# Squares and half of the Newton products of the first stage moved from ScalarE and VectorE to GpSimd

## The reference

```
def sensitivity(r, mu, sigma):
    return jnp.exp(-(1.0 / r - 1.0 / mu) ** 2 / (2.0 * sigma * sigma))   # MU = 1, SIGMA = 0.5
msg     = z @ W + B                                   # z: layer norm of x
sens    = sensitivity(dist_matrix, MU, SIGMA)         # dist_matrix: adj, 1354 x 1354
weights = jnp.where(dist_matrix < CUTOFF, sens, 0.0)  # CUTOFF = 1
x1      = x + weights @ msg
```

## Time and profile before

| | |
|---|---|
| median of three runs | 573.3 us |
| profiled execution | 573.15 us |
| its span, first to last instruction | 571.4 us |
| mean granted TensorE clock | 0.94 |
| busy over the span | PE 492.5, VectorE 387.3, ScalarE 271.6, GpSimd 118.1 us |
| first sum added to x (L1402) | 42.61 us |
| first gates turned (L1481) | 59.45 us |

### The profile page before, as it was taken

One profiled execution on the slowest core, in us unless ns is written; L12 is line 12 of the kernel. 1 busy time (PEld: TensorE's weight loads), 2 busy tenths in 40 slices (PEclk: granted clock), 3 DMA queues, 4 the chain that ended last, 5 costly groups with the idle time before them and its releaser, 6 DMA issues.

```text
span 571.4 us, 6186 instructions
## 1 busy us (share of the span) xinstructions
PE 492.5 (86%) x1889; PEld 306.4 (54%) x1889; DVE 387.3 (68%) x715; ACT 271.6 (48%) x445; POOL 118.1 (21%) x181
## 2 busy tenths in 40 slices
PE   5564879677879999999889998998978799999997
PEld 4322535344546645455444443445545687788896
DVE  2989987756586722267568868778856966666664
ACT  5988694758765421222422122111236544454553
POOL 3000000000010000000000058730103455555554
PEclk9696699889799999999999998999988999999999
DMA  8960000000000010000000013210000000000000
GB/s 284 317 170 1 1 0 0 1 1 0 1 1 1 5 45 1 0 2 0 1 0 1 28 49 103 65 30 1 0 5 2 0 2 0 20 1 2 19 1 13
DMA packets 13076, 16.76 MB, mean 29 GB/s; under 512 B 2007, under 2 KB 8410, under 8 KB 13038
## 3 DMA queue, kind: packets, MB, share of 16 engines
q1 hardware_dynamic: 13038, 16.30, 9.1%
HBM read 15.60 MB, written 0.69 MB: 29 GB/s over the span
## 4 chain that ended last, share of the span: by engine, by line
PE 56%; DVE 24%; ACT 10%; issue 8%; POOL 1%; DVEq 0%; POOLq 0%; ACTq 0%
PE bank L1220 9%; PE bank L886 7%; PE bank L888 7%; PE bank L887 7%; PE bank L1050 4%; PE bank L1168 3%; DVE pr_ring L1818 3%; PE bank L1019 2%; PE bank L1209 2%; DVE y_units L1379 2%; DVE y_units L1368 2%; PE bank L915 2%; DVE t_units L1374 2%; DVE hr_ring L1634 2%; DVE y_units L1389 1%
## 5 line engine op out<-in xcount | busy, mean ns | idle before, releaser
L1220 PE MATMUL bank<-pr_ring,hW 128*128 128x512 f32 (+3 forms) x198 | 95.5, 568 | 7.2 <-DVE pr_ring L1818 6.7
L1818 DVE SCALAR_TENSOR_TENSOR pr_ring<-adjT,regR,bank 128x512 f32<-128x512 f32 (+3 forms) x99 | 64.9, 680 | 29.5 <-PE bank L1209 27.8
L1929 DVE TENSOR_TENSOR adjT<-adjT,bank 128x512 f32<-128x512 f32 (+1 forms) x66 | 41.2, 624 | 45.5 <-PE bank L1324 24.0
L866 ACT ACTIVATE adjT<-bank 128x512 f32<-128x512 f32 (+1 forms) x66 | 36.2, 549 | 54.1 <-PE bank L888 54.1
L886 PE MATMUL bank<-z3hi,w13hi 128*128 128x512 f32 (+4 forms) x132 | 50.8, 385 | 8.2 <-DVE pr_ring L1933 3.2
L1220 PEld LDWEIGHTS bank<-pr_ring,hW 128*128 128x128 f32 (+1 forms) x198 | 35.7, 197 | 37.0 <-issue 17.8
L915 PE MATMUL bank<-y_units,msg 128*128 128x512 f32 (+3 forms) x66 | 33.3, 638 | 20.5 <-DVE y_units L1389 20.5
L888 PE MATMUL bank<-z3hi,w13lo 128*128 128x512 f32 (+4 forms) x132 | 49.4, 374 | 0.0
L887 PE MATMUL bank<-z3lo,w13hi 128*128 128x512 f32 (+4 forms) x132 | 49.0, 371 | 0.0
L1019 PE MATMUL bank<-hr_ring,W2s 128*128 128x512 f32 (+1 forms) x96 | 46.2, 569 | 0.0
L548 POOL TENSOR_TENSOR prr_ring<-adjT,adjTr 128x512 fp32r<-128x512 f32 (+4 forms) x34 | 36.0, 1060 | 48.8 <-ACT adjTr L858 46.8
(11 more groups left out here) (272 smaller groups left out, 1039.3 us busy)
## 6 DMA issues: line engine op xcount, KB each, us to landing
stage<-in_w SPq DMA_DIRECT2D x8, 341.0 KB, 3.0
adjT<-in_adjT SPq DMA_DIRECT2D x1, 2560.0 KB
adjT<-in_adjT SPq DMA_DIRECT2D x1, 1650.0 KB
adjT<-in_adjT SPq DMA_DIRECT2D x3, 512.0 KB, 5.7
adjT<-in_adjT SPq DMA_DIRECT2D x1, 1024.0 KB
W1f<-in_W SPq DMA_DIRECT2D x1, 1024.0 KB, 11.9
stage<-in_w SPq DMA_DIRECT2D x3, 256.0 KB
xT<-in_xT SPq DMA_DIRECT2D x1, 677.0 KB, 3.8
```

Of the source, the lines that this page charges most:

```text
L866: nc.scalar.activation(s1_buf(q)[0:r, 0:w], B_H1[q % 2][0:r, 0:w], ACT.Silu).then_inc(s["s_silu"], 1)
L1220: nc.tensor.matmul(B_ACC[:, 0:w], hW[0:r, j, k * P:(k + 1) * P], ring[0:r, 0:w], start=(k == 0 and j == 0), stop=(k == K - 1 and j == T - ...
L1818: nc.vector.scalar_tensor_tensor(out=pr_ring[0:r, 4 + p % R_RING, 0:w], in0=adjT[0:r, j, cols(c)], scalar=g_col[0:r, j, k:k + 1], in1=B_F[ ...
L1929: nc.vector.tensor_tensor(sg, sg, B_GATE1[n % 2][0:r, 0:w], ALU.mult).then_inc(s["s_gated"], 1)
```

## The change

GpSimd takes the squares of units 2 to 17, as a product of the adjacency with itself (L520 of the new kernel), and the products t = r*y of the eight units 2, 4, ..., 16 (L526). ScalarE keeps the squares of units 0 and 1, VectorE the products of units 0, 1 and the odd ones. The logarithm of a unit waits for GpSimd's square, and the Newton step of an even unit for GpSimd's product. GpSimd's 24 new instructions stand in one fixed order between its constants and its diagonals. In ScalarE's and VectorE's straight code the order of the tasks is written anew, with unit 6 now taken ahead of `x1(0)`; in the tables the entries "sq" and the even "mult" are gone and nothing else moves.

```
+OWN = 2
+def on_pool(g):
+    return g >= OWN and g % 2 == 0
...
 ACT0 = {
-    0: [("sq", 9), ("ln", 9), ("arg", 7), ("exp", 7), ("inv", 9)], 2: [("arg", 8), ("sq", 10), ("ln", 10), ("inv", 10)], 3: [("exp", 8)],
+    0: [("ln", 9), ("arg", 7), ("exp", 7), ("inv", 9)], 2: [("arg", 8), ("ln", 10), ("inv", 10)], 3: [("exp", 8)], 4: [("arg", 9), ("exp", 9)],
...
 DVE0 = {
-    0: [("sign", 8), ("cut", 7), ("mult", 8)], 1: [("step", 8), ("sign", 9)], 2: [("v",), ("mult", 9)], 3: [("step", 9), ("cut", 8)],
+    0: [("sign", 8), ("cut", 7)], 1: [("step", 8), ("sign", 9)], 2: [("v",), ("mult", 9)], 3: [("step", 9), ("cut", 8)],
...
+            def square(g):                     # GpSimd
+                c, a, _ = unit(g)
+                if c:
+                    at(pool, f"adjT_in{c}", 32)
+                elif a < 6:
+                    at(pool, f"adjT_first{a // 2}", 16)
+                else:
+                    at(pool, "adjT_in0", 32)
+                at(pool, "gnn_mm", g - RINGY + 1)
+                pool.tensor_tensor(unit_y(g), unit_adj(g), unit_adj(g), ALU.mult).then_inc(s["pool_sq"], 1)
+            def product(g):
+                pool.wait_ge(s["newton_s"], g + 1)
+                at(pool, "newton_y", g - RINGT + 1)
+                pool.tensor_tensor(unit_t(g), unit_adj(g), unit_y(g), ALU.mult).then_inc(s["newton_p"], 1)
+            square(2)
+            square(3)
+            square(4)
+            product(2)
+            square(5)
...
+            square(16)
+            square(17)
+            product(16)
...
             def rec_log(g):
-                act.wait_ge(s["rec_sq"], g + 1)
+                if g < OWN:
+                    act.wait_ge(s["rec_sq"], g + 1)
+                else:
+                    act.wait_ge(s["pool_sq"], g - OWN + 1)
...
             def newton_step(g):
-                at(dve, "newton_t", g + 1)
+                if on_pool(g):
+                    at(dve, "newton_p", g // 2)
+                else:
+                    at(dve, "newton_t", (g + 3) // 2)
```

More of the change, by code:

```diff
@@ L117 @@
[L117 to L121, removed]
@@ new lines @@
+    9: [("cut", 11), ("step", 12)], 10: [("sign", 13), ("mult", 13)], 11: [("x1", 1), ("center", 1, 1), ("step", 13)], 13: [("scale", 1, 1)],
+    15: [("rank", 1), ("sign", 14), ("turn", 1)], 16: [("cut", 12)], 17: [("cut", 13), ("x2", 0)], 18: [("step", 14), ("sign", 15)],
+    19: [("center", 2, 0), ("mult", 15), ("step", 15), ("sign", 16)], 20: [("cut", 14), ("step", 16)], 21: [("cut", 15), ("sign", 17), ("mult", 17)],
+    22: [("scale", 2, 0), ("step", 17), ("cut", 16)], 23: [("diag", 0), ("cut", 17)], 25: [("x1", 2), ("center", 1, 2), ("diag", 1)],
@@ L506, in _ @@
             pool.tensor_copy(GT0[:, :, :].rearrange("p i n -> p (i n)"), zero[:, 0:1].to_broadcast([P, 2 * CW])).then_inc(s["pad_zero"], 1)
+            def square(g):
[17 more added lines that the diff above has]
+            square(5)
+            square(6)
+            product(4)
+            square(7)
+            square(8)
+            product(6)
+            square(9)
+            product(8)
+            square(10)
+            square(11)
+            product(10)
+            square(12)
+            square(13)
+            product(12)
+            square(14)
+            square(15)
+            product(14)
+            square(16)
+            square(17)
+            product(16)
             pool.wait_ge(s["w_ready"], UNITS)
@@ L1610, in weights_low @@
                 nc.vector.tensor_tensor(W1lo[:, half, :], W1f[:, half, :], W1hi[:, half, :].bitcast(F32), ALU.subtract).then_inc(s["W1_lo"], 1)
[L1612 removed]
+            side(("sign", 0))
+            side(("mult", 0))
+            side(("step", 0))
+            side(("sign", 1))
+            side(("mult", 1))
+            side(("step", 1))
+            rows_step(0)
+            side(("sign", 2))
+            rows_step(1)
+            message(0)
+            side(("sign", 3))
+            side(("mult", 3))
+            message(1)
+            side(("step", 2))
+            message(2)
+            side(("cut", 0))
+            side(("step", 3))
+            side(("sign", 4))
+            side(("cut", 1))
+            side(("sign", 5))
+            side(("mult", 5))
+            side(("cut", 2))
+            dve.wait_ge(s["gate_in"], 32)
+            nc.vector.tensor_tensor(gate_bias[:, 0, :], gate_bias[:, 0, :], gate_bias[:, 1, :], ALU.add).then_inc(s["bgs_set"], 1)
+            side(("step", 4))
+            side(("step", 5))
+            side(("cut", 3))
+            side(("sign", 6))
+            dve.wait_ge(s["ffn0_in"], 80)
+            nc.vector.tensor_copy(b2hi[:, :], b2x[:, :]).then_inc(s["b2_split"], 1)
+            side(("cut", 4))
+            at(dve, "b2_split", 1)
+            nc.vector.tensor_tensor(b2lo[:, :], b2x[:, :], b2hi[:, :].bitcast(F32), ALU.subtract).then_inc(s["b2_split"], 1)
+            side(("cut", 5))
+            side(("step", 6))
             weights_low(0)
[L1614 to L1615 removed]
+            side(("x1", 0))
+            side(("center", 1, 0))
             weights_low(1)
[L1617 to L1625 removed]
+            side(("sign", 7))
+            side(("mult", 7))
+            side(("scale", 1, 0))
+            side(("cut", 6))
+            side(("rank", 0))
+            side(("step", 7))
+            side(("turn", 0))
             for q in range(TILES0):
```

153 lines of the change are left out of this document (48 added, 105 removed).

## The result

| | before | after |
|---|---|---|
| median on one chip (4 runs each) | 572.85 us (571.27 to 574.38) | 595.44 us (594.51 to 596.06) |
| ratio | | 1.0365, 95% interval 1.0323 to 1.0407 |
| profiled execution, its span | 573.15, 571.4 us | 596.06, 594.2 us |
| mean granted TensorE clock | 0.94 | 0.918 |
| `x1(0)` (L1402, now L1438) | 42.61 us | 60.09 us |

The change makes the kernel 3.65% slower. Of the 22.8 us that the span grew, 17.5 are there at `x1(0)` and 20.3 at `x1(2)`; the last 2.5 come behind `x1(2)`, where both kernels do the same. This last part stays unexplained.

A forecast was written before the change was run, and what follows sets the result against it. The prediction took VectorE to bound the first stage, with slack of some 20 us in the tiles. It summed 573.15 + 23 up to `x1(0)` + 4 in the tiles = 600.2 us, said as 600, range 585 to 613.

The forecast's parts named there:

- The mechanism: GpSimd instructions reading SBUF and VectorE instructions with two SBUF inputs take turns, each waiting out the other; 600 us, chance 0.6.
- Price of one GpSimd instruction: On GpSimd, 2.2 us per 1024-column instruction, 1.15 for 512 columns, 1.45 for 660, 0.8 for 330.
- The walk to `x1(0)`: First stage, instruction by instruction in turns: `x1(0)` comes at 65.6 us instead of 42.61, 23 us later.
- The order: Unit 6 and one W1lo ahead of `x1(0)` add 3.4 us, waits 2 us more; unit 6 done earlier gives nothing.
- `x1(0)` to the gates: Chain over layer norm and router up to the first tile has the same instructions, so the 23 us stay.
- The tiles: 62.4 to 146.1 us: net 6 us more in VectorE's queue, a third absorbed by slack, so + 4 us.
- The sum: Whole kernel: 573.15 + 23 + 4 = 600.2 us, said as 600.
- VectorE keeps its turn: Rival: GpSimd cannot enter between back-to-back VectorE instructions, so squares 7, 8 and 9 slip behind; 588 us, chance 0.2.
- Slower GpSimd: Rival: 2.45 us per GpSimd instruction and hardly any slack in the tiles; 610 us, chance 0.11.
- Each at its own speed: Rival: the hold does not apply here, so VectorE is relieved; 571 us at best, chance 0.09.
- The relief of ScalarE brings nothing: First stage: taking squares off ScalarE, 1.05 us each at 1024 columns, gains nothing; ScalarE now waits for GpSimd's squares.

The follow-up runs named there:

- order_alone: Changed kernel with all squares back on ScalarE and even products back on VectorE, only the rewritten order left; 581.72 us, 1.011 times the kernel before.
- change_again: The changed kernel measured and profiled once more, unaltered, on another chip; 594.98 us, 1.0347 times the kernel before.
- idle_fresh: Kernel before plus six unneeded GpSimd squares of 128x1024, each waiting for a VectorE sign; 586.59 us, before 574.33.
- idle_products: Kernel before, same order, plus ten GpSimd products of 128x1024 that nothing needs; 590.55 us, 1.0222 times the kernel before.
- products_alone: Changed kernel in the new order with all squares back on ScalarE, even products still on GpSimd; 583.41 us, 1.01 times the kernel before.
- both_old_order: Changed kernel with GpSimd's whole part, but ScalarE's and VectorE's straight code in the order of before; 593.11 us, 1.032 times the kernel before.
- late_squares: Kernel before with only the squares of units 12 to 17 moved to GpSimd; 576.06 us, 1.0023 times the kernel before.
- late_both: Kernel before with squares of units 12 to 17 and products of 12, 14 and 16 moved to GpSimd; 574.95 us, 0.999 times the kernel before.

## Why the prediction was right, step by step

**The mechanism: shown.** Slower, by turns, with the waits inside the durations of 1.2 and 2.8 us side by side; L1603 and L1668 unchanged. Idle products alone bring it about (1.0222), memsets don't (1.0005), and taking GpSimd's work out takes the holds out (order_alone).

**Price of one GpSimd instruction: too high.** This is the term that was mis-sized. I took 2.2 us for each. A square holds 1.58 us and a product of two tensors 2.08, and eight of the eleven ahead of `x1(0)` are squares. (The order of GpSimd's queue shows eleven instructions ahead of the product of unit 8; where the section on the change says ten, eleven is right, and the walk counts eleven.) They cost 15.7 us over eleven, 1.43 each; I had 22 less the 2.2 that messages hide. The nearest rows had two different inputs or other shapes; none was a tensor with itself, and a duration alone is more than what the other engine loses.

**The walk to `x1(0)`: 65.6 said, 60.1 measured.** 15.7 of holds, 2.44 of waiting for ScalarE in front of sign 6 (3.8 said), 3.4 of unit 6 and W1lo, less 2.3 of products and less the 2.05 us that before waited in front of `x1(0)` and a cut: 17.2, against 17.5 measured. The walk gave every square its turn at once, and no price to the loads behind square 3. In the trace GpSimd waited 4.32 us for a load before square 3, which came at 15.93 instead of 15.0, beside product 1, and 5.67 us for one before square 6. Square 6 then took 5.25 us from 33.13 while three VectorE instructions ran undisturbed beside it (33.68 to 36.62), and the product of unit 4 took 3.77.

**The order: priced roughly right, its return missed.** Unit 6 ahead of `x1(0)` was in the walk with 3.4 + 2 us and "gives nothing" after. order_alone shows 9.7 us at `x1(0)` (of them 5.05 in one wait) and 5.0 of them back by `x1(1)`, part of it perhaps by the clock.

**`x1(0)` to the gates:** unchanged said, 17.34 instead of 16.84 us measured.

**The tiles: + 4 said, + 2.3 and + 0.4 measured from the gates to `x1(2)` in the two profiles, and not for the reasons given.** Gates to `x1(1)` is 37.8 us before, 34.2 with the order alone, 40.9 with everything (39.9 in change_again): the order brings some 3.7 and GpSimd's work costs some 6 to 7, the effect of the clock included in both. I had priced only holds, and the order at nothing. The trace adds waits for the products: 3.8 us in front of the steps of units 8 and 10, the idle time of L1415 in the groups above. The table leaves VectorE some 1.7 us of other work between sign and step of unit 8, and none for unit 10, while the product takes GpSimd 2.2 us and its turn.

**The sum: nearer than its terms.** 600.2 said and 596.06 profiled are 4.1 apart. The first stage was 5.5 too long and the tiles 1.7, and 0.5 behind `x1(0)` and 2.5 behind `x1(2)`, where nothing was forecast, cover 3.0 of that by luck.

**The rivals.** *VectorE keeps its turn* fails in idle_fresh and idle_products, though GpSimd was passed over at square 6 and at product 4 in the changed kernel; squares 7 and 8 (from 42.07) and square 9 (55.41) did go in ahead of `x1(0)`. Its `x1(0)`, 42.61 + 14.5 = 57.1, was nearer to 60.1 than mine, though, for its lower price of an instruction and not for its mechanism. *Slower GpSimd* fails: 1.89 and 2.18 us alone. *Each at its own speed* fails on the first row at 2.80 us. "The relief of ScalarE brings nothing" fits the first stage, where ScalarE stood idle 9.05 us waiting for VectorE's step of unit 4 (to 45.08), but no run tests it by itself.

**Open.** Why GpSimd's instruction took 3.7 to 5.5 us in some places (33.13 and 38.34 here; 31.01 in products_alone; 33.97 in both_old_order), passed over by VectorE instructions, while idle work always alternated. Square 6's recorded start follows a load's landing and may be early; product 4's does not. And why the parts add up to less than the whole. At `x1(0)` they do add up: 9.7 for the order, 8.3 more for the squares and 0.0 for the products, against 17.5. In the tiles they don't: 3.0 and 0.2 us over order_alone from the gates to `x1(1)`, against 6.8 (5.7 in change_again). The coupling of squares and products is one candidate, TensorE's clock another; neither was tested. Nor is it known what sets the 2 to 3 us behind `x1(2)`.

## What to carry to other kernels

Before moving elementwise work from a full VectorE to an idle GpSimd, look at what each side reads: if both have SBUF inputs (two on VectorE), the engines take turns, and a GpSimd instruction costs VectorE nearly its own full duration, here 1.6 to 2.1 us, to save 1.2 or, for a square, nothing. Where VectorE had slack (late_squares, late_both) this brought neither loss nor gain. Memsets, which only write, and VectorE work with a bank as an input went beside it free. To see the hold, compare the mean of a group with its undisturbed value; it is not in the idle columns. And if two kinds of work share GpSimd's one queue, see which moments the queue's order ties the second kind to.

## What the hardware showed that I had not expected

- A product of a tensor with itself took GpSimd 1.89 us at 128x1024, of two tensors 2.18; they hold VectorE 1.58 and 2.08 us.
- The hold doesn't scale with the held instruction: 128x8 took 2.14 instead of 0.15 us, 128x11 1.85 instead of 0.16.
- With both queues full the engines alternate one by one, and both get slower: ten products 25.67 instead of 18.9 us, VectorE's 1.22 us instructions 2.80.
- 24 memsets of 512 KB, 24.15 us of a busy GpSimd, cost nothing measurable.
